# A transformer layer on eight cores: the load of the output-projection weights moved from the V-transpose stage to the attention block's start

## Chip, cores, metric
The kernel runs on all 8 cores of one Trainium2 chip. Each core runs the same program on its own 2048 tokens, with no exchange between cores. The metric is device time in microseconds of the slowest core.

## What is computed
One pre-norm transformer layer on x of shape (2, 8192, 2048): 16 heads of 128, rotary positions, attention within a window of 512, and an FFN of width 8192. The reference, cut:

```python
# attention on layernorm(x)
q, k, v = (einsum('bsi,oi->bso', xn, W) for W in (Wq, Wk, Wv))   # per head, 128 wide
q, k = _rope(q, cos, sin), _rope(k, cos, sin)
scores = einsum('bhnid,bhnjd->bhnij', qb, kw) * scale            # blocks of 512, keys of this and the previous block
base = (j > i) & (j <= i + WIN)
attn = softmax(where(mask, scores, -inf))
out = einsum('bhnij,bhnjd->bhnid', attn, vw)
x = x + einsum('bsi,oi->bso', out, Wo)
# FFN on layernorm(x)
D = gelu(X @ W0.T + bias0); x = x + (D @ W1.T + bias1)
```

## The kernel before
Each core works on 2048 own tokens plus 512 of context before them (CTX = 2560). The program is a row of blocks, each with code for the five engines, and each opened by `barrier`, which all five engines must reach. Within a block engines meet by counting semaphores. The blocks are:

- p0: layer norm of x and its transpose into `ln1T`.
- p1: projections Q, K and V (matmul at L370), spilled to HBM as `q_sp`, `k_sp` and `vT_sp`.
- p1t: the V-transpose stage (from L544). V was made transposed; here it is turned back. The 20 tiles of 128 tokens come in five groups (`sg4`) of four. GpSimd loads a group's 16 pieces of `vT_sp` into `vtl[sg4 % 2]` (L569); for groups 2 to 4 it first waits (`sTpV`) until TensorE is through with the group two before. TensorE waits for a group's 16 loads, then does 16 transposes per tile into `ptpv` (L606). ScalarE copies a tile to `vstage[st % 2]`, after the store of two tiles before has landed (`sSpVa`, `sSpVb`). SP stores the tile to `v_sp` (L586).
- p2: attention and output projection in four blocks (`qb`) of 512 tokens. Per block 64 steps of scores, exponential (ScalarE), scaling by the reciprocal and copy of the transposed result (VectorE), and product with V; then the projection with `wo_sb` (L799), the residual and the second layer norm. TensorE waits for `sRing` at the start of each block (10 DMAs: 4 for `kring`, 2 for `qring`, 4 for `vring`), and for `sWo2` (four wo loads) only after the attention of block 0.
- p3: the FFN in two stages (L1057, L1202), with weights streamed by GpSimd.

GpSimd issues its DMAs in program order on one queue; SP has another, and both run on the same 16 DMA engines. In p1t the function `wo_msk_load(g)` is called after group 1's vtl loads. It issues the mask load and four loads of `wo_t`, each 2 MB as written (bf16) and 4 MB as read (f32). `ring_kq(g, 0)` follows, then the vtl loads of groups 2 to 4, then `ring_v(g, 0)`. `wo_sb` and the rings have their own place in SBUF through p1t and p2. `DO_V` is true, so GpSimd in p2 issues only the ring loads of blocks 1 to 3, each after the attention of the block before (`sQbPE`).

Of the kernel before, what the change touches and what calls it, by code (L numbers as in the profile page):

```python
# [32 lines left out]
def build_nc():  # L33
# [3 lines left out]
    def dram_in(name, shape, dtype=F32):  # L37
        return nc.dram_tensor(name, shape, dtype, kind="ExternalInput").ap()
# [16 lines left out]
    msk_in = dram_in("msk", [128, 5 * 640], BF16)  # L55
# [24 lines left out]

    _wmap = {"q": wq_t, "ka": wk_t, "kb": wk_t, "va": wv_t, "vb": wv_t}
    WLOADS = [(_wmap[nm], oh) for nm, _, _, _ in SWEEPS for oh in range(2)]
    W1P = [0, 0]
    for li in range(len(WLOADS)):
# [4 lines left out]
    with ctx:  # L89
# [24 lines left out]
        sem = {n: e(nc.semaphore(n)) for n in semnames}  # L114
# [4 lines left out]
        def barrier(eng):  # L119
            eng.sem_inc(sem["sBar"], 1)  # L120
            eng.wait_ge(sem["sBar"], NENG * bar_n[0])
# [82 lines left out]
        with pA:  # L204
# [17 lines left out]
            with p0:  # L222
# [8 lines left out]
                with nc.Block() as blk:  # L231
                    @blk.sync
                    def _(s):
                        barrier(s)
                        s.dma_start(idm[:], idm_in).then_inc(sem["sMisc"], 16)
                        s.dma_start(ccs[:], cc_in).then_inc(sem["sMisc"], 16)
                        s.dma_start(sss[:], ss_in).then_inc(sem["sMisc"], 16)
                        for t in range(NT0):
                            if t >= 4:
                                s.wait_ge(sem["sLn1"], t - 3)  # L240
                            s.dma_start(xb[t % 4][:],
                                        x_ctx[t * 128:(t + 1) * 128, :]
                                        ).then_inc(sem[xsem[t % 4]], 16)
# [266 lines left out]
        msk = p2o.enter_context(nc.sbuf_tensor("msk_s", [128, 5 * 640], BF16))  # L510
# [5 lines left out]
        def ring_kq(g, qb):  # L516
            for o0 in range(0, 16, 4):
                g.dma_start(
                    kring[:, o0 * 1024:(o0 + 4) * 1024].rearrange(
                        "p (o c) -> p o c", c=1024),  # L520
                    k_spv[:, o0: o0 + 4, qb * 512: qb * 512 + 1024]
                ).then_inc(sem["sRing"], 16)
            for o0 in range(0, 16, 8):
                g.dma_start(
                    qring[:, o0 * 512:(o0 + 8) * 512].rearrange(
                        "p (o c) -> p o c", c=512),
                    q_spv[:, o0: o0 + 8, qb * 512:(qb + 1) * 512]
                ).then_inc(sem["sRing"], 16)

        def ring_v(g, qb):  # L530
            for j0 in range(0, 8, 2):
                g.dma_start(
                    vring[:, j0 * 2048:(j0 + 2) * 2048].rearrange(
                        "p (j f) -> p j f", f=2048),
                    v_spv[:, qb * 4 + j0: qb * 4 + j0 + 2, :]
                ).then_inc(sem["sRing"], 16)

        def wo_msk_load(g):
            g.dma_start(msk[:], msk_in).then_inc(sem["sMsk"], 16)
            for i0 in range(0, 16, 4):  # L540
                g.dma_start(
                    wo_sb[:, i0 * 2048:(i0 + 4) * 2048].rearrange(
                        "p (i f) -> p i f", f=2048),
                    wo_tv[:, i0: i0 + 4, :]  # L544
                ).then_inc(sem["sWo2"], 16)

        if DO_V:
            p1t = ExitStack()
            with p1t:
                vtl = [p1t.enter_context(  # L550
                    nc.sbuf_tensor(f"vtl{j}", [128, 16 * 512], BF16))
                    for j in range(2)]
                vstage = [p1t.enter_context(
                    nc.sbuf_tensor(f"vstage{j}", [128, 2048], BF16))
                    for j in range(2)]
                ptpv = [p1t.enter_context(
                    nc.psum_tensor(f"ptpv{j}", [128, 2048], BF16))
                    for j in range(2)]
                bar_n[0] += 1
                with nc.Block() as blk:  # L560
                    @blk.gpsimd
                    def _(g):
                        barrier(g)
                        for sg4 in range(5):
                            if sg4 >= 2:
                                g.wait_ge(sem["sTpV"], 4 * (sg4 - 1))
                            vs = sem["sVta" if sg4 % 2 == 0 else "sVtb"]
                            for o in range(16):
                                g.dma_start(  # L569
                                    vtl[sg4 % 2][:, o * 512:(o + 1) * 512],  # L570
                                    vT_sp[o * 128:(o + 1) * 128,
                                          sg4 * 512:(sg4 + 1) * 512]
                                ).then_inc(vs, 16)
                            if sg4 == 1:
                                wo_msk_load(g)
                                ring_kq(g, 0)
                        g.wait_ge(sem["sSpVa"], 16 * 4)
                        g.wait_ge(sem["sSpVb"], 16 * 4)
                        ring_v(g, 0)

                    @blk.sync
                    def _(s):
                        barrier(s)
                        for st in range(20):
                            s.wait_ge(sem["sEvV"], st + 1)
                            s.dma_start(  # L586
                                v_sp[st * 128:(st + 1) * 128, :],
                                vstage[st % 2][:]
                            ).then_inc(
                                sem["sSpVa" if st % 2 == 0 else "sSpVb"], 16)  # L590
                        s.wait_ge(sem["sSpVa"], 16 * 10)
                        s.wait_ge(sem["sSpVb"], 16 * 10)

                    @blk.tensor
                    def _(tn):
                        barrier(tn)
                        for sg4 in range(5):
                            tn.wait_ge(sem["sVta" if sg4 % 2 == 0 else "sVtb"],
                                       16 * 16 * (sg4 // 2 + 1))
                            for st4 in range(4):  # L600
                                st = sg4 * 4 + st4
                                if st >= 2:
                                    tn.wait_ge(sem["sEvV"], st - 1)
                                ins = None
                                for o in range(16):
                                    ins = tn.transpose(  # L606
                                        ptpv[st % 2][:, o * 128:(o + 1) * 128],
                                        vtl[sg4 % 2][:, o * 512 + st4 * 128:
                                                     o * 512 + (st4 + 1) * 128],
                                        idm[:])  # L610
                                ins.then_inc(sem["sTpV"], 1)

                    @blk.scalar
                    def _(scraw):
                        barrier(scraw)
                        sc = _AW(scraw)
                        for st in range(20):
                            sc.wait_ge(sem["sTpV"], st + 1)
                            if st >= 2:
                                sc.wait_ge(  # L620
                                    sem["sSpVa" if st % 2 == 0 else "sSpVb"],
                                    16 * (st // 2))
                            sc.copy(vstage[st % 2][:], ptpv[st % 2][:])
                            sc.sig(sem["sEvV"])

                    @blk.vector
                    def _(vraw):
                        barrier(vraw)
# [4 lines left out]
        with p2:  # L633
# [30 lines left out]
            with nc.Block() as blk:  # L664
# [34 lines left out]
                @blk.gpsimd  # L699
                def _(g):  # L700
                    barrier(g)
                    if not DO_V:
                        wo_msk_load(g)
                        ring_kq(g, 0)
                        ring_v(g, 0)
                    for qb in range(1, NQB):
                        g.wait_ge(sem["sQbPE"], qb)
                        ring_kq(g, qb)
                        ring_v(g, qb)
# [614 lines left out]
```

## Time and profile before

| what | us |
|---|---|
| runs of the kernel | 3915.23, 4255.12, 4403.44 (median 4255.12) |
| profiled execution | 3900.29 |
| its span, slowest core (3) | 3898.7 |
| spans of the eight cores | 3867.5 to 3898.7 |
| TensorE matmul busy | 3279.2 (84%) |
| VectorE, ScalarE busy | 786.2 each (20%) |
| GpSimd busy | 593.0 (15%) |

Read it so: one execution, core 3, times from the span's start. "PE" is TensorE's matmul, "PEld" its weight load. DMA share is the mean busy share of the core's 16 DMA engines; GB/s is what they wrote, so a load that turns f32 into bf16 counts with its bf16 bytes.

### The profile page before, as it was taken

Reading aid. Unit: us, or ns where it says so; the run is one execution under the profiler, and the core shown is the slowest. Engines: PE = TensorE matmul, PEld = TensorE weight load, DVE = VectorE, ACT = ScalarE, POOL = GpSimd, SP = SyncE. Lnnn points to the kernel's source line nnn. Section 1 sums busy time; section 2 is a strip of 40 time slices with the busy share of each in tenths; the row PEclk is TensorE's granted clock in tenths of the full one; section 3 lists DMA queues with packets and bytes.
Section 4 is the critical chain, followed back from the end, with each engine's and each line's share of the span. In section 5 each row is a group of like instructions: output and inputs, shape, how many; then the busy total and the mean of one; then the engine's idle time right before and its main releaser. Section 6 shows DMA issues by size and latency. Waiting matters only on the chain. (4 is left out here: it accounts for less than half of the span.)

```text
span 3898.7 us, 47168 instructions; the slowest of 8 cores (3867.5 to 3898.7 us)
## 1 busy us (share of the span) xinstructions
PE 3279.2 (84%) x17600; PEld 1633.4 (42%) x17600; DVE 786.2 (20%) x1618; ACT 786.2 (20%) x1285; POOL 593.0 (15%) x933
## 2 busy tenths in 40 slices
PE   1599999997157667676839999999997999999999
PEld 1344444443144353535424444444443444444444
DVE  5555554000024443434430000000000000000000
ACT  3355454111143241414201111111110000000000
POOL 1000101002110000000000000001203433343321
PEclk9999999998578888888859999999998999999999
DMA  9322555543931406050163333332807989889764
GB/s 234 102 62 62 101 103 106 99 86 95 232 130 55 163 1 216 1 189 28 60 167 76 81 81 81 81 78 62 152 39 178 223 200 223 211 218 225 189 198 126
DMA packets 191858, 488.96 MB, mean 125 GB/s; under 512 B 21776, under 2 KB 54544, under 8 KB 188816
## 3 DMA queue, kind: packets, MB, share of 16 engines
q0 software_dynamic: 132304, 304.97, 37.5%
q1 hardware_dynamic: 59328, 180.97, 14.0%
q8 instruction: 143, 2.34, 0.2%
q14 instruction: 83, 0.68, 0.1%
HBM read 487.96 MB, written 115.34 MB: 155 GB/s over the span
## 5 line engine op out<-in xcount | busy, mean ns | idle before, releaser
L1202 PE MATMUL pool<-w1q,gq 128*128 128x512 bf16 x4096 | 903.7, 382 | 42.0 <-DMA gq<-g_sp 38.5
L1057 PE MATMUL pool<-ln2T,w0b 128*128 128x512 bf16 x4096 | 886.2, 380 | 2.0 <-PEq L120 2.0
L370 PE MATMUL pool<-ln1T,wbuf 128*128 128x512 bf16 x3584 | 777.2, 380 | 6.6 <-PE pool L370 4.7
L1202 PEld LDWEIGHTS pool<-w1q,gq 128*128 128x128 bf16 x4096 | 397.6, 98 | 531.8 <-issue 68.7
L1057 PEld LDWEIGHTS pool<-ln2T,w0b 128*128 128x128 bf16 x4096 | 401.2, 98 | 486.9 <-issue 5.0
L370 PEld LDWEIGHTS pool<-ln1T,wbuf 128*128 128x128 bf16 x3584 | 350.5, 98 | 433.2 <-issue 13.8
L144 DVE TENSOR_TENSOR obuf<-pool,yh 128x512 f32<-128x512 f32 x64 | 44.3, 692 | 1806.1 <-PE pool L1206 1674.2
L1133 POOL DMA_DIRECT2D gq<-g_sp x256 | 225.4, 901 | 760.2 <-PE pool L1206 568.7
L170 ACT ACTIVATE gst<-pool,bias_s 128x2048 bf16<-128x2048 f32 x64 | 125.9, 1967 | 745.1 <-PE pool L1057 745.1
L799 PE MATMUL pool<-wo_sb,outT 128*128 128x512 bf16 x1024 | 238.8, 397 | 29.0 <-DVE ybuf L903 25.0
L828 ACT ACTIVATE expb<-pool 128x640 bf16<-128x640 f32 x256 | 180.2, 705 | 278.1 <-PE pool L742 275.2
L775 PE MATMUL ppv<-expT,vring 128*128 128x128 bf16 x1280 | 102.9, 248 | 117.2 <-DVE expT L870 117.2
L144 DVE RECIPROCAL rec<-sums 128x1 f32<-128x1 f32 x256 | 41.1, 160 | 699.6 <-ACT expb L828 697.1
L799 PEld LDWEIGHTS pool<-wo_sb,outT 128*128 128x128 bf16 x1024 | 102.6, 101 | 164.2 <-issue 55.9
L757 PE MATMUL ptp<-idm_s,expb 128*128 128x128 bf16 x1280 | 131.0, 241 | 44.6 <-DVE expT L870 40.4
L170 ACT COPY e2b<-pool 64x512 f32<-64x512 f32 x288 | 166.9, 580 | 6.9
L1028 POOL DMA_DIRECT2D w0b<-w_t x112 | 59.3, 605 | 676.6 <-PE pool L1057 614.7
L606 PE MATMUL ptpv<-idm_s,vtl 128*128 128x128 bf16 x320 | 33.9, 292 | 134.2 <-DMA vtl<-vT_sp 85.4
L144 DVE TENSOR_TENSOR tt<-e1b,ccs 128x512 bf16<-128x512 f32 x144 | 99.7, 692 | 219.2 <-ACTq L164 186.8
L775 PEld LDWEIGHTS ppv<-expT,vring 128*128 128x128 bf16 x1280 | 90.7, 112 | 126.7 <-issue 126.7
L314 PE MATMUL ptr<-idm_s,lnb 128*128 128x128 bf16 x320 | 37.3, 309 | 119.5 <-ACTq L164 119.5
L170 ACT COPY e1b<-pool 128x512 f32<-128x512 f32 x144 | 84.3, 585 | 231.3 <-PE pool L370 190.0
(59 smaller groups left out, 1969.3 us busy)
## 6 DMA issues: line engine op xcount, KB each, us to landing
gq<-g_sp POOLq DMA_DIRECT2D x256, 512.0 KB, 12.1
w0b<-w_t POOLq DMA_DIRECT2D x128, 256.0 KB, 16.4
g_sp<-gst SPq DMA_DIRECT2D x64, 512.0 KB, 2.6
w1q<-w_t POOLq DMA_DIRECT2D x256, 128.0 KB, 19.6
xb<-x_ctx SPq DMA_DIRECT2D x20, 1024.0 KB, 11.4
wbuf<-wk_t POOLq DMA_DIRECT2D x64, 256.0 KB, 17.5
wbuf<-wv_t POOLq DMA_DIRECT2D x64, 256.0 KB, 18.0
kring<-k_sp POOLq DMA_DIRECT2D x16, 1024.0 KB, 13.6
```

The costliest lines, as they stand in the source:

```text
L144: ins = fn(*a, **k)
L170: ins = fn(*a, **k)
L314: ins = tn.transpose(ptr[r][:, jj * 128:(jj + 1) * 128], lnb[t % 2][:, ic * 128:(ic + 1) * 128], idm[:])
L370: ins = tn.matmul(pool[:, slot * 2048 + k * 512: slot * 2048 + (k + 1) * 512], lhs, ln1T[:, roff: roff + 512], start=(i == 0), stop=(i == ...
L757: ins = tn.transpose(ptp[tp_slot][:, j * 128:(j + 1) * 128], expb[eb][:, j * 128:(j + 1) * 128], idm[:])
L775: ins = tn.matmul(pv[:, qx * 128:(qx + 1) * 128], vt, expT[hh % 2][:, col: col + 128], start=(jc == qx), stop=(jc == qx + 4))
L799: ins = tn.matmul(pool[:, hf * 1024 + col * 512: hf * 1024 + (col + 1) * 512], lhs, wo_sb[:, w0c: w0c + 512], start=(hx == 0), stop=(hx == ...
L828: scraw.activation(expb[eb][:], pool[:, ps_slot * 1024: ps_slot * 1024 + 640], AF.Exp, scale=SCALE, accum_out=sums[:, eb: eb + 1]).then_in ...
L1028: g.dma_start(w0b[ng % 2][:, i * 1024:(i + 1) * 1024], w0_t[i * 128:(i + 1) * 128, ng * 1024:(ng + 1) * 1024]).then_inc(ws, 16)
L1057: ins = tn.matmul(pool[:, slot * 2048 + scv * 512: slot * 2048 + (scv + 1) * 512], lhs, ln2T[:, i * TOWN + scv * 512: i * TOWN + (scv + 1) ...
L1133: g.dma_start(dstv[:, grp * 8:(grp + 1) * 8, :], gsrc).then_inc(gsem, 16)
L1202: tn.matmul(pp, lhs, w1q[hq4 % 2][:, n * 512: (n + 1) * 512], start=(n == 0), stop=False)
```

## The change
The mask load stays where it was. The four wo loads leave the V-transpose stage and become the first DMAs that GpSimd issues in the block p2, behind its barrier and ahead of the ring loads of block 1. `wo_msk_load` becomes `wo_load`, with the wo loop alone. No wait is added or removed, and nothing else changes.

```diff
-        def wo_msk_load(g):
-            g.dma_start(msk[:], msk_in).then_inc(sem["sMsk"], 16)
+        def wo_load(g):
             for i0 in range(0, 16, 4):
                 g.dma_start(
                     wo_sb[:, i0 * 2048:(i0 + 4) * 2048].rearrange(
@@ p1t, gpsimd
                             if sg4 == 1:
-                                wo_msk_load(g)
+                                g.dma_start(msk[:], msk_in).then_inc(
+                                    sem["sMsk"], 16)
                                 ring_kq(g, 0)
@@ p2, gpsimd
                     barrier(g)
                     if not DO_V:
-                        wo_msk_load(g)
+                        g.dma_start(msk[:], msk_in).then_inc(sem["sMsk"], 16)
                         ring_kq(g, 0)
                         ring_v(g, 0)
+                    wo_load(g)
                     for qb in range(1, NQB):
                         g.wait_ge(sem["sQbPE"], qb)
                         ring_kq(g, qb)
```

## Rows read from the trace of the kernel before

**Rows 1.** Medians of the two dies: span and mean granted TensorE clock.
```profile
die 0 (median of its cores): 3877.6 us, clock 0.935
die 1 (median of its cores): 3884.8 us, clock 0.932
```

**Rows 2.** The page's 40 slices of the span, in tenths.
```profile
PE   1599999997157667676839999999997999999999
...
DMA  9322555543931406050163333332807989889764
```

**Rows 3.** Timeline of TensorE, 925 to 1120: start, us, what [idle before <-releaser].
```profile
1063.05 3.57 PE L606 MATMUL ptpv<-idm_s,vtl 128*128 128x128 bf16 x32 [68.22 <-DMA vtl<-vT_sp]
...
1115.37 0.58 PE L727 MATMUL pool<-msk_s,idm_s 128*128 128x512 bf16 x1 [6.53 <-PEq L120]
```

**Rows 4.** Timeline of POOL (its DMA issues), 925 to 1120.
```profile
963.25 3.07 POOL L541 DMA_DIRECT2D wo_sb<-wo_t  x4
966.20 3.11 POOL L518 DMA_DIRECT2D kring<-k_sp  x4
...
970.94 8.67 POOL L569 DMA_DIRECT2D vtl<-vT_sp  x16
995.36 8.47 POOL L569 DMA_DIRECT2D vtl<-vT_sp  x16 [15.76 <-PE ptpv L606]
```

**Rows 5.** Issue and landing by line: msk, the last two wo, vtl group 2.
```profile
L539 POOL DMA_DIRECT2D msk_s<-msk x1: 607/607/607, 962.7 to 962.7; - x1
...
DMA to landing us min/median/max: 8.2/8.2/8.2
...
L541 POOL DMA_DIRECT2D wo_sb<-wo_t x2: 845/849/853, 964.7 to 965.5; - x2
...
DMA to landing us min/median/max: 57.4/63.8/70.3
...
L569 POOL DMA_DIRECT2D vtl<-vT_sp x16: 681/691/702, 970.9 to 978.9; - x16
...
DMA to landing us min/median/max: 82.7/83.3/83.9
```

**Rows 6.** Stretches: us, busy of PE, PEld, DVE, ACT, POOL, clock, DMA share, GB/s.
```profile
945.00:1063.00 118.00, 13.95 (x128) 12.38 (x128) 0.00 (x0) 16.20 (x9) 42.27 (x75) 0.51 0.98 227
...
1036.00:1063.00 27.00, 0.00 (x0) 0.00 (x0) 0.00 (x0) 0.00 (x0) 0.00 (x0) 0.50 1.00 315
```

**Rows 7.** Stores of vstage: 1002 to 1008, landings of all 20; ScalarE's copy after the hole.
```profile
L586 SPq DMA_DIRECT2D v_sp<-vstage x2: 319/319/319, 1002.3 to 1007.1; - x2
...
DMA to landing us min/median/max: 11.1/11.2/11.3
...
DMA to landing us min/median/max: 2.6/8.6/12.6
...
1065.06 1.86 ACT L170 COPY vstage<-ptpv 128x2048 bf16<-128x2048 bf16 x1 [58.14 <-PE ptpv L606]
```

**Rows 8.** SP's DMA queue, 960 to 1060: packets, MB, share of 16 engines.
```profile
q1 hardware_dynamic: 1152, 4.19, 11.1%
```

**Rows 9.** Timeline of TensorE, first output projection of block 0.
```profile
1247.90 4.29 PE L799 MATMUL pool<-wo_sb,outT 128*128 128x512 bf16 x10 [0.93 <-ACT outT L816]
```

**Rows 10.** Stretches after p1t; the instruction queues of 1120 to 1247, then of 3500 to 3600.
```profile
1120.00:1247.00 127.00, 87.66 (x947) 65.63 (x944) 58.48 (x189) 54.86 (x139) 0.00 (x0) 0.92 0.01 2
...
3500.00:3600.00 100.00, 100.00 (x459) 44.00 (x457) 4.84 (x7) 0.00 (x0) 42.30 (x64) 1.00 0.96 226
...
q8 instruction: 8, 0.13, 0.4%
q14 instruction: 6, 0.05, 0.1%
...
q8 instruction: 3, 0.05, 0.2%
```

**Rows 11.** VectorE's first operation in attention.
```profile
1118.94 0.16 DVE L144 RECIPROCAL rec<-sums 128x1 f32<-128x1 f32 x1 [450.68 <-ACT expb L828]
```

## Prediction
> **What bounds the kernel now.** I read the spans of the cores first, to see that no die is disturbed. The medians of the dies are 3877.6 and 3884.8 us at a clock of 0.935 and 0.932 [rows 1], so core 3, the slowest with 3898.7, can stand for all. Then the page's 40 slices: TensorE is busy to nine tenths nearly everywhere, and the deepest hole after the start is the eleventh slice (975 to 1072 us), where PE stands at 1 and the DMA row at 9 [rows 2]. The transpose stage of V (941 to 1115 us) lies around it, and the diff changes what is queued there.
>
> The timeline of TensorE in that stage shows the hole itself. The transposes of V get through groups 0 and 1 and then stand still for 68.22 us until 1063.05, released by a load of vtl. Attention starts at 1115.37 [rows 3]. Outside the hole the tiles go at the pace of the two-buffer rotation of the stores, whose landings take 2.6 to 12.6 us [rows 7].
>
> Next, what stands ahead of that vtl in the GpSimd queue. The timeline of POOL gives the order of issue: the four wo loads at 963.25, then kring (and, between, qring), and only then vtl of group 2 at 970.94 [rows 4]. The landings follow the same order. msk lands at 962.7 + 8.2 = 970.9 us; the last two wo loads at 964.7 + 57.4 = 1022.1 and 965.5 + 70.3 = 1035.8; vtl of group 2 last at 978.9 + 83.9 = 1062.8 [rows 5]. The DMA engines are busy all the time: share 0.98 from 945 to 1063 [rows 6]. They are what limits this stretch, and wo is in front.
>
> **What the change takes out of the stage.** Four DMAs (8.39 MB written as bf16, so 16.78 MB read as f32) leave the queue between msk and kring. I want the DMA time that is wo's own, without the stores that shared the engines meanwhile. The last store before the hole was issued at 1007.1 and landed about 11 us later [rows 7], so the last wo piece, from 1022.1 to 1035.8, ran alone: 13.7 us for 4.19 MB read. Four of them are 4 x 13.7 = 54.8 us. As a check from the other side: after wo, kring, qring and vtl of group 2 needed 1062.8 - 1035.8 = 27.0 us with no store beside them. In the changed order they start at 970.9 and share the engines with the stores. Eight stores moved 4.19 MB, and the stretch 960 to 1060 gives their queue 11.1% of 100 us [rows 8], so 11.1 us in all, some 2 of it before 970.9. That gives 970.9 + 27.0 + 9 = 1007 us for group 2, against 1063: 56 us. The two agree; I take 55.
>
> The Trainium skill would price wo otherwise: "HBM Reference", section "Specifications", gives a core about 358 GB/s when its neighbour streams too, which makes 16.78 MB an estimated 47 us and the kernel's time 3853 us. The alone piece ran at 4.19 MB / 13.7 us = 306 GB/s, so the trace has it slower than the page's share.
>
> **Bounds of that saving.** Above: wo held the queue from 970.9 to 1035.8, that is 64.9 us, if the stores in that time had cost nothing. Below: the next limit is the store rotation. Group 2's first copy needs the landing of the seventh store, issued at 1002.25 and landed near 1013.6 (11.3 us); its copy came at 1065.06 and took 1.86 [rows 7]. With stores no faster than beside wo, the gain is 1065.1 - 1013.6 = 51 us, and the second copy (1065.06 + 1.86 + 0.3 = 1067.2 against 1007.1 + 11.1 = 1018.2) makes it 49. The median over all 20 stores is 8.6 us, less than the 11 beside wo, so I keep 49 as the lower end only.
>
> **What stays in the stage.** msk, kring, qring and all of vtl keep their order. vtl of group 3 waits for the transposes of group 1, so it was issued at 995.36 [rows 4]; that is before 1007, so it still queues directly behind group 2. From group 2 on the traffic is the same as before, and I move the rest rigidly: attention starts at 1115.4 - 55 = 1060 us.
>
> **What the change adds.** The four wo loads are now the first thing POOL does in the attention block, at about 1060 us. Their issue takes 3.07 us [rows 4]. Only ring loads of block 1 are queued behind them, and those wait for the end of attention anyway. By their own rate they land at 1060 + 1 + 54.8 + a little for two xh loads of SP = about 1120 us. wo is first read at 1247.90 in the old time [rows 9], 1193 in the new. The cover is the attention of block 0, 132.5 us long, in which the DMA engines are at 0.01 of their time [rows 10]. The slack is some 70 us, so I cost the move at nothing. Without that cover it would cost its 55 us back.
>
> Does attention get slower with a stream of loads beside it? No row has attention and heavy loads together. The nearest row is the second FFN stage, where the DMA share is 0.96 and TensorE is busy for 100.0 of 100 us [rows 10]. So TensorE's work as such isn't slowed, which speaks for 0 as the lower bound; the upper one is 68 us, from the fetch rival below. I take 0, since the FFN row is the one with that traffic.
>
> **The sum.** The profiled execution: span 3898.7 us, 3900.3 with what lies around it. 3898.7 - 55 + 1.6 = 3845 us, which is 1.4% less. By the bounds 65 and 49 it is 3835 to 3851. The median of the three runs shown, 4255, is far above the profile and the lowest is 3915.2; I forecast for the profile's condition, so the low run would put the same saving at 3860.
>
> **Rivals.**
> Forecast, 0.80: 49 to 65 us are gained, 3835 to 3851.
> Part of the gain is lost, 0.09: the stage finds another limit before 1007 us is reached, or attention gives some of it back. For it speaks that the stores' rotation (49 us) is only a few us behind the loads (55 us). Against it speaks that all after group 2 is unchanged. Half lost is 3872.
> Nothing comes of it, 0.03: the loads of kring and vtl take up the time, as if all eight cores' reads were the limit. Then they would run slower than the 315 GB/s of 1036 to 1063 [rows 6]. 3900.
> Instruction fetches held up, 0.05, the case on the other side: in the 127 us of attention the instruction queues moved 14 packets [rows 10], about 6 in the 55 us of the load. A store that lands in 2.6 us at best needed 11 beside wo [rows 7], so a fetch could come 8.5 us later. 6 x 8.5 = 51 us would eat nearly the whole gain, and if 8 fetches are held it is 68, 13 us slower than before: 3913. It decides from 55 / 8.5 = 6.5 fetches. Against it: in the FFN stretch, 3 and more fetches at DMA share 0.96 cost PE nothing.
> wo comes late, 0.03: only if landing takes over 133 us from the start of attention, that is if the load runs at 40% of its rate; 3900 at 188 us. The Trainium skill names a cause ("SBUF — State Buffer", the "DVE blocks DMA" trap): VectorE in a two-port mode keeps GpSimd from writing descriptors, about 620 ns becoming 3100. By that factor the issue would be an estimated 15 us and the time unchanged at 3845 us. No row here has this overlap: VectorE's first operation comes 3.6 us after TensorE's first in attention [rows 11], when the issue is about over.
>
> **Range and chances.** The forecast's own range, 3835 to 3851, widened by the 15 us by which 3900.3 and 3915.2 differ, is 3820 to 3866. I reach to the half-lost case: 3822 to 3880, which leaves out about 0.15. A measurement of this kernel tells a difference of about 2%, 78 us, from none. Even the whole 68.2 us of the wait is less than that, so faster by over 2% is only left for the spread of executions: 0.06. Within 2%: 0.90. Slower by over 2% needs 133 us given back in attention: 0.04.
>
> **What would show it.** Right: POOL has no wo issue before the attention block; the wait for vtl of group 2 is 5 to 20 us, ended near 1007; attention starts near 1060 and its block 0 lasts 131 to 134 us; the wo loads land 55 to 62 us after their issue; everything later is earlier by the same 55. Wrong: TensorE idle with "issue" or its sequencer named in 1060 to 1120; a wait on wo before the first output projection; kring landing later than 22 us after msk; group 2's start released by ScalarE or the stores and not by vtl.

## The result and the profile after

The changed kernel takes 3856.85 us (median of 10 runs, lowest 3845.18) against 3918.63 us before (10 runs, lowest 3892.24). In some runs the cores of one die or of both (cores 0 to 3, 4 to 7) get a lower clock and take longer; the medians include four such runs of before and two of after, the ratios leave them out, and where a profile fell in such a run (e_six, e_double) I use the other die. The ratio is 0.9874, with a 95% interval of 0.9829 to 0.9918: 1.3% faster, between 0.8% and 1.7%. In us it is 49.3 (the means of the runs compared are 3908.0 and 3858.7). By the bound of 2% used in the prediction it counts as the same: the interval shows that there is a gain, and also that it is smaller than that bound. The profiled execution took 3855.9 us against 3900.3, 44 us less, with both dies alike:

```profile
die 0 (median of its cores): 3829.6 us, clock 0.940
die 1 (median of its cores): 3843.3 us, clock 0.937
```

Lines of the kernel after are those of core 3, the core of the rows of before, unless another core is named. First the timeline of TensorE in the V-transpose stage, which answers to [rows 3]:

```profile
956.60 3.57 PE L606 MATMUL ptpv<-idm_s,vtl 128*128 128x128 bf16 x32 [16.87 <-DMA vtl<-vT_sp]
...
1009.03 3.57 PE L606 MATMUL ptpv<-idm_s,vtl 128*128 128x128 bf16 x32 [20.45 <-DMA vtl<-vT_sp]
```

The wait for group 2 is down from 68.22 to 20.45 us, with the same releaser, and group 2 starts at 1009.03 in place of 1063.05. The timeline of POOL shows what was moved [rows 4]:

```profile
961.72 0.61 POOL L574 DMA_DIRECT2D msk_s<-msk  x1
962.24 3.07 POOL L518 DMA_DIRECT2D kring<-k_sp  x4
965.22 1.85 POOL L524 DMA_DIRECT2D qring<-q_sp  x2
966.97 8.63 POOL L568 DMA_DIRECT2D vtl<-vT_sp  x16
...
1064.76 2.98 POOL L540 DMA_DIRECT2D wo_sb<-wo_t  x4 [36.62 <-PEq L120]
```

The landings, by line (issue in us from the start, then min/median/max to landing) [rows 5]:

```profile
L574 POOL DMA_DIRECT2D msk_s<-msk x1: 607/607/607, 961.7 to 961.7; - x1
...
DMA to landing us min/median/max: 10.9/10.9/10.9
...
L568 POOL DMA_DIRECT2D vtl<-vT_sp x16: 637/652/664, 967.0 to 974.9; - x16
...
DMA to landing us min/median/max: 29.8/30.5/33.8
...
L540 POOL DMA_DIRECT2D wo_sb<-wo_t x4: 742/765/780, 1064.8 to 1067.0; - x4
...
DMA to landing us min/median/max: 20.5/38.0/55.1
```

vtl of group 2 lands at 974.9 + 33.8 = 1008.7, and wo at 1067.0 + 55.1 = 1122.1, some 76 us before TensorE first reads it at 1198.5. The stretches of the attention of block 0, with the wo loads beside it and without (us, busy of PE, PEld, DVE, ACT, POOL, clock, DMA share, GB/s) [rows 10]:

```profile
1065.00:1122.00 57.00, 41.62 (x403) 30.73 (x402) 24.83 (x81) 26.04 (x64) 2.74 (x4) 0.84 0.97 167
1122.00:1198.00 76.00, 51.06 (x560) 38.15 (x556) 34.63 (x112) 32.26 (x82) 0.00 (x0) 0.92 0.01 1
```

In the first stretch the DMA engines are full (0.97), and TensorE still does 403 matmuls in 57 us. On core 6 the granted clock of this stretch is 0.84 in both kernels. For the kernel before, the same stretch counted from the start of attention on core 6 (1119 to 1175, 56 us, DMA share 0.06) has 394 matmuls; the kernel after on core 6 (1059 to 1115, DMA share 0.97) has 395. On core 3 itself the kernel before had 411 matmuls in the like stretch (1116 to 1173), but at a granted clock of 0.92 against 0.84 after. These are the two lines of core 6, before and after:

```profile
1119.00:1175.00 56.00, 40.71 (x394) 29.92 (x395) 23.65 (x78) 25.11 (x61) 0.00 (x0) 0.84 0.06 20
```

```profile
1059.00:1115.00 56.00, 40.66 (x395) 29.95 (x393) 23.86 (x78) 25.38 (x63) 2.53 (x4) 0.84 0.97 170
```

To compare kernels below I use the medians over the eight cores of four marks, each the start of a first matmul, in us from the start of the span:

| kernel | group 2 | attention (first on kring) | first wo matmul | between the last two |
|---|---|---|---|---|
| before | 1062.2 | 1115.7 | 1249.2 | 133.1 |
| after | 1009.3 | 1064.4 | 1197.5 | 133.9 |
| difference | 52.9 | 51.3 | 51.7 | |

The start of the first FFN stage moves by 49.3 us (2046.5 to 1997.2), of the second by 51.7 us, and the median of the cores' last matmuls by 46.8 us. So most of the gain made in the V stage reaches the end, give or take a few us by which the later stages differ between executions.

What ends the stage, in both kernels, is the last store of V. On core 3 of the kernel after it is issued at 1060.9 and lands 2.9 us later, at 1063.8:

```profile
L586 SPq DMA_DIRECT2D v_sp<-vstage x1: 319/319/319, 1060.9 to 1060.9; - x1
...
DMA to landing us min/median/max: 2.9/2.9/2.9
```

The first matmul of the attention block (on the mask) starts at 1064.72. On the eight cores it comes 0.9 to 1.5 us after that landing, and vring has landed 10 us or more before. Before, on core 3, the last store landed at 1111.6 + 2.6 = 1114.2, and that matmul started at 1115.37.

### The profile page after: what moved, and what is told of

It is laid out like the page before. It is cut to its first block and busy times, and to the rows that moved or that the text cites. A ratio compares the mean times of both kernels' runs of the same rounds, so it can differ in the third digit from the quotient of the medians.

```text
span 3854.3 us, 47168 instructions; the slowest of 8 cores (3822.0 to 3854.3 us)
## 1 busy us (share of the span) xinstructions
PE 3279.7 (85%) x17600; PEld 1634.8 (42%) x17600; DVE 786.1 (20%) x1618; ACT 786.5 (20%) x1285; POOL 592.9 (15%) x933
## 5 line engine op out<-in xcount | busy, mean ns | idle before, releaser
L370 PEld LDWEIGHTS pool<-ln1T,wbuf 128*128 128x128 bf16 x3584 | 350.5, 98 | 433.1 <-issue 13.7
L728 PE MATMUL pool<-msk_s,idm_s 128*128 128x128 bf16 (+1 forms) x256 | 77.3, 302 | 60.1 <-DVE ybuf L904 29.2
```

The lines of the kernel that those rows point to most:

```text
L370: ins = tn.matmul(pool[:, slot * 2048 + k * 512: slot * 2048 + (k + 1) * 512], lhs, ln1T[:, roff: roff + 512], start=(i == 0), stop=(i == ...
L728: tn.matmul(pool[:, c0: c0 + mw], idm[:], mask_cols(qb, qc, 0), start=True, stop=False)
```

## Experiments

For e_six and e_double the cores of die 1 are used, against the same cores of before (group 2 at 1063.3, attention block 133.4 us) and after (attention block 133.8 us).

### e_half and e_six: what a wo load costs in the stage

Two of the four loads stay:

```diff
+                                wo_load(g, 0, 8)      # p1t, behind msk
-                    wo_load(g)
+                    wo_load(g, 8, 16)                 # p2
```

> Edit: two of the four wo loads stay in the V-transpose stage, two go to the attention block. Medians over the eight cores so far: start of the transposes of group 2 at 1062.2 us before, 1009.3 after; first attention step on kring 1115.5 and 1064.4. Theory A (the stage is limited by the DMA engines' work, and each piece costs its own share): group 2 at 1009.3 + 2 x 13.2 = 1036 us, attention at 1090. Theory B (the gain comes only when the queue ahead of group 2 is short enough, since the store rotation waits too): the first two pieces cost less than half, group 2 before 1028. Theory C (what counts is that nothing large stands in front, not how much): group 2 after 1045.

Group 2 starts at 1036.9 and attention at 1090.3; on core 2:

```profile
1035.65 3.21 PE L607 MATMUL ptpv<-idm_s,vtl 128*128 128x128 bf16 x32 [42.06 <-DMA vtl<-vT_sp]
```

From four to two pieces gains 25.3 us, from two to none 27.6. Theory A said 1036. No threshold shows: each piece costs about its own share. The run whose trace is read took 3883.9 us, between the two kernels.

The other way, two pieces more in the kernel before:

```diff
                                 wo_msk_load(g)
+                                for i0 in range(0, 8, 4):
+                                    g.dma_start(vring[...], wo_tv[:, i0: i0 + 4, :]
+                                    ).then_inc(sem["sDg"], 16)
                                 ring_kq(g, 0)
```

GpSimd waits for the two before it loads vring anew.

> Edit: the kernel before, with two more loads of the same kind (2 MB bf16 written, 4 MB f32 read each, into vring, which is loaded anew later) behind the four wo loads. No store shares the DMA engines by then, so this prices a piece alone. If a piece's own work is the 13.7 us that the prediction took from the last landing, group 2 starts at 1062.2 + 27.4 = 1089.6 us; if it is 12.7 us (a quarter of the 51 us that the queue's packets took in the kernel after), at 1087.6; if the stores' rotation were a limit beside it, less than 1085.

On core 5 the wait grows from 66.93 to 93.86 us:

```profile
1087.62 3.57 PE L614 MATMUL ptpv<-idm_s,vtl 128*128 128x128 bf16 x32 [93.86 <-DMA vtl<-vT_sp]
```

The median of die 1 goes from 1063.3 to 1086.8, 23.5 us for two pieces, or 11.8 each by the starts; by the waits of the four cores, which grow by 26.8, 26.9, 22.1 and 25.5 us, it is 11.1 to 13.5 each. The cores scatter by more than the two values that the expectation wanted to tell apart (12.7 and 13.7). The landings of the two added pieces settle it better. On core 5 the fourth wo load lands at 1034.8, and then:

```profile
L577 POOL DMA_DIRECT2D vring<-wo_t x2: 877/882/887, 965.0 to 965.8; - x2
...
DMA to landing us min/median/max: 82.8/88.9/94.9
```

That is 1047.8 and 1060.7, so 13.0 and 12.9 us for a piece with no store beside it. On the four cores of die 1 the two take 12.3 to 13.5 us each, 12.9 in the median. So the price goes on past four pieces, at 12.9 and not 13.7 a piece.

### e_double and e_mid: does the load cost anything beside attention

The four loads twice, one after the other, so that the stream lasts twice as long:

```diff
                     wo_load(g)
+                    g.wait_ge(sem["sWo2"], 4 * 16)
+                    wo_load(g)
@@ tensor, block 0
-                            tn.wait_ge(sem["sWo2"], 4 * 16)
+                            tn.wait_ge(sem["sWo2"], 8 * 16)
```

> Edit: the kernel after, with all four wo loads issued a second time in the attention block when the first four have landed, and the first output projection waiting for both. So some 105 of the 133 us of attention of block 0 have the DMA engines full. Theory A (attention takes nothing from the loads beside it): from the first kring matmul to the first wo matmul 132 to 135 us on the median core, as before (133.6) and after (133.3). Theory B (instruction fetches come late behind wo packets, 8.5 us each): the second 50 us hold up some 6 more, 20 to 50 us longer. Theory C (VectorE and ScalarE slowed a little by the stream): 2 to 5 us longer.

Attention to the first wo matmul takes 132.9 us on die 1 (133.8 with four loads, 133.4 with none), and 132.2 over all cores. The stretch on core 5, with the DMA engines full for 105 us:

```profile
1065.00:1170.00 105.00, 72.45 (x787) 53.63 (x786) 49.13 (x160) 48.65 (x121) 5.32 (x8) 0.92 0.98 163
```

The same 105 us of the kernel before on this core (1117 to 1222) had 761 matmuls at a DMA share of 0.04; the granted clock was 0.88 there and 0.92 here, so the two aren't quite like for like. On core 4 (1063 to 1168, and 1115 to 1220 before) it is 756 (clock 0.89) against 760 (0.92). So neither late instruction fetches nor a slower VectorE or ScalarE shows; theory A holds.

The loads in the middle of attention:

```diff
+                    g.wait_ge(sem["sExpN"], 12)
                     wo_load(g)
```

> Edit: the kernel after, with GpSimd waiting for the 12th scaled exponential before it issues the wo loads, so that VectorE is at work in its fast modes during the issue, and the loads come some 25 us later. Theory A (no lock worth the name): each issue takes 0.74 to 0.85 us, the loads last 50 to 53 us and are done some 50 us before the projection; attention 132 to 135 us. Theory B (VectorE keeps GpSimd from writing descriptors): issues of over 2 us each, first landing over 25 us after the issue; the end is still in time, so the kernel's time is the same.

On core 5 the issue starts at 1089.45, with VectorE at work:

```profile
L540 POOL DMA_DIRECT2D wo_sb<-wo_t x4: 740/756/770, 1089.5 to 1091.7; - x4
DMA to landing us min/median/max: 17.4/34.9/51.4
```

Each issue takes 0.74 to 0.77 us, as in the kernel after (0.742 to 0.780), and the last load lands 51.4 us after its issue. Attention to the first wo matmul takes 132.1 us, and the one run took 3846.0 us, within the runs of the kernel after. VectorE kept nobody waiting. The test is a mild one: in the 2.97 us of the four issues VectorE ran two scalings of 0.39 and 0.46 us, besides reciprocals and copies from PSUM, and the profile doesn't show its mode, so a hold-up as short as one such operation could pass unseen.

### e_nocover: the same loads with no work to hide them

```diff
-                    wo_load(g)
                     for qb in range(1, NQB):
                         g.wait_ge(sem["sQbPE"], qb)
+                        if qb == 1:
+                            wo_load(g)
```

> Edit: the kernel after, with the wo loads issued only when the attention of block 0 is through, ahead of the ring loads of block 1. Nothing covers them. Theory A (the move is free only for the cover, as the prediction says): group 2 at 1009 and attention at 1064 as in the kernel after, but TensorE waits some 52 us for wo, first wo matmul on the median core at 1197.6 + 50 = 1248 to 1252 us, and the kernel is back at the time of before, about 3905 us. Theory B (the gain was not the load's place but less crowding in the V stage): first wo matmul before 1230.

Group 2 and attention start as in the kernel after (1010.8 and 1064.2), the first wo matmul at 1250.5, and the one run took 3909.8 us. Core 3 waits:

```profile
PE pool L801 <- DMA wo_sb<-wo_t: 55.2, 1, 55.2
```

So the less crowded V stage alone is worth nothing at the end; the gain is the cover that attention gives. This agrees with the prediction's price for the case without it.

### e_tail and e_tail2: could the loads have stayed in the V stage, behind everything else

```diff
                         ring_v(g, 0)
+                        wo_load(g)          # p1t, last; e_tail2: two of the four
@@ p2
-                    wo_load(g)              # e_tail2: the other two
```

> Edit: the wo loads stay in the V-transpose stage, but as the last DMAs that GpSimd issues there, behind vring. Theory A (the later stores of V share the engines with wo, and land in some 11 us instead of 2.6 to 9.9): group 2 at 1009 as in the kernel after, attention 5 to 12 us later than its 1064.4. Theory B (the engines are idle enough by then, 0.85 busy): attention within 2 us of 1064.4, so that the place behind the barrier brings nothing of its own. wo lands near 1085 in both, long before the projection.

Neither theory was near for the start of attention. Group 2 starts at 1011.8, but attention at 1118.3, 54 us after the kernel after, and the one run took 3908.8 us. Core 3:

```profile
1117.42 0.59 PE L728 MATMUL pool<-msk_s,idm_s 128*128 128x512 bf16 x1 [60.64 <-PEq L120]
```

```profile
L540 POOL DMA_DIRECT2D wo_sb<-wo_t x4: 760/780/792, 1030.2 to 1032.4; - x4
DMA to landing us min/median/max: 41.4/63.3/81.5
```

```profile
L587 SPq DMA_DIRECT2D v_sp<-vstage x1: 320/320/320, 1070.6 to 1070.6; - x1
...
DMA to landing us min/median/max: 10.8/10.8/10.8
```

The last store landed at 1070.6 + 10.8 = 1081.4, and no instruction of the program waits for wo there. Yet TensorE sat 60.64 us, until 3.5 us after the last wo load had landed (1032.4 + 81.5 = 1113.9). On all eight cores the first kring matmul comes 3.9 to 4.2 us after that landing. So I formed another theory, that the end of a block waits for all that GpSimd's queue was given, and tried it with two loads there.

> Edit: two wo loads behind vring in the V-transpose stage, two at the start of the attention block. With all four behind vring, attention did not start until 3.9 to 4.2 us after the last wo load had landed, on each of the eight cores, though the last store had landed some 40 us before. Theory A (the end of a block waits until all that GpSimd's queue was given has landed): the second of the two loads lands near 1086 us, attention starts 4 us after it on every core, near 1090, as when the two stood ahead of kring (1090.3). Theory B (the stores of the last V tiles are what is late): attention follows the last store, near 1078 to 1082, before or without regard to the landing of wo.

```profile
L540 POOL DMA_DIRECT2D wo_sb<-wo_t x2: 760/768/775, 1030.6 to 1031.4; - x2
DMA to landing us min/median/max: 39.8/47.0/54.3
```

On core 3 the second load lands at 1031.4 + 54.3 = 1085.7 and attention starts at 1089.7. Per core, landing of the second load and first kring matmul:

| core | 0 | 1 | 2 | 3 | 4 | 5 | 6 | 7 |
|---|---|---|---|---|---|---|---|---|
| landing | 1086.2 | 1086.2 | 1086.4 | 1085.7 | 1083.5 | 1086.1 | 1086.1 | 1088.7 |
| attention | 1090.3 | 1090.1 | 1090.4 | 1089.7 | 1087.4 | 1090.1 | 1090.1 | 1092.6 |
| later by | 4.1 | 3.9 | 4.0 | 4.0 | 3.9 | 4.0 | 4.0 | 3.9 |

Theory A of e_tail2 holds, within 0.1 us of 4.0, over a spread of 5 us in the landings. The one run took 3879.4 us. That the loads had to go behind the block's barrier, and not only to the back of the queue, was not seen in the prediction. It is what makes this change worth something: with e_half's two pieces at the front and with e_tail2's at the back, attention starts at the same 1090.

### e_kqlate, e_kqsplit, e_three: what limits the rest of the stage

The 20.45 us wait that is left looks like the next gain. First, kring and qring moved behind all of vtl:

```diff
                             if sg4 == 1:
                                 g.dma_start(msk[:], msk_in)...
-                                ring_kq(g, 0)
+                        ring_kq(g, 0)       # after group 4's vtl, ahead of vring
```

> Edit: the kernel after, with the kring and qring loads of block 0 moved behind the vtl loads of group 4, ahead of vring. The wait of 17 to 23 us before group 2 should go. Theory A (the stage is limited by the DMA engines' total work, of which this removes nothing; they are busy 0.96 and 0.85 of the two halves of the stage): attention starts at most 5 to 8 us earlier than 1064.4, and the vring loads land later. Theory B (the wait itself is the cost): attention at 1045 to 1048, 17 us faster. Theory C: the rings land after the last store and attention waits for them, 0 to 10 us slower.

The long wait is gone (after the first wait, of some 17 us at 956, no core waits for vtl before 1002 us, and then for at most 4.67 us, on core 0), and attention starts at 1065.1: nothing gained (the time's ratio to before is 0.9843, 0.9788 to 0.9898, which can't be told from 0.9874). vring now lands late; on core 0:

```profile
L532 POOL DMA_DIRECT2D vring<-v_sp x4: 696/708/716, 1011.9 to 1014.0; - x4
DMA to landing us min/median/max: 34.3/41.1/46.2
```

It lands at 1060.2, and attention starts at 1064.0, 3.8 us later, by the rule found above; on the eight cores it is 3.8 to 4.0 us. The wait wandered from group 2 to the end of the stage. The bytes of the stage are the same, and though group 2 starts 22 us earlier (987.3), the last store lands only 3 us earlier on the median core (1059.9 against 1062.9).

Second, fewer bytes: the rings of heads 8 to 15 (3.1 MB) moved to the attention block.

```diff
-                                ring_kq(g, 0)
+                                ring_kq(g, 0, (0, 8))
@@ p2
+                    ring_kq(g, 0, (8, 16), "sRc")
                     wo_load(g)
@@ tensor
+                                if qb == 0 and step == 32:
+                                    tn.wait_ge(sem["sRc"], 16 * 3)
```

> Edit: the kernel after, with the loads of kring and qring for heads 8 to 15 of block 0 (3.1 MB) moved to the attention block, ahead of wo; TensorE waits for them at head 8. Theory A (DMA work in the stage is what counts): 3.1 MB at the 308 GB/s of kring, qring and vtl is 10 us less work; attention starts at 1054 to 1056, and the kernel is 8 to 10 us faster than after. Theory B (the store rotation is the next limit): 3 to 5 us. Heads 8 to 15 are not waited for: they land some 12 us after the start and are needed at 66 us.

Attention starts at 1055.2, 9.2 us earlier than after, as theory A has it. The time's ratio to before is 0.9834 (0.9778 to 0.9890), too wide to tell it from the kernel after by itself.

Third, `vstage` with three buffers in place of two.

> Edit: the kernel after with three vstage buffers in place of two. Theory A (DMA work limits the stage up to its last stores): group 2 starts within 2 us of 1009, attention 0 to 4 us earlier. Theory B (the rotation of the stores paces the tiles of groups 2 to 4): attention 8 us or more earlier.

Attention starts at 1059.5, 4.9 us earlier, with group 2 at 1009.5. That lies between the theories: the rotation costs a few us, and not the 8 of theory B. But here the limit has changed. The last store lands 6.1 us earlier than in the kernel after (1056.8 on the median core), and attention follows the landing of vring by 3.8 to 3.9 us on all eight cores. On core 3 vring lands at 1028.3 + 28.1 = 1056.4 and the first kring matmul comes at 1060.25:

```profile
L532 POOL DMA_DIRECT2D vring<-v_sp x4: 696/712/723, 1026.2 to 1028.3; - x4
...
DMA to landing us min/median/max: 14.6/21.4/28.1
```

So the end of the block took back about 1 us of what the third buffer gave.

### e_best: both together

```diff
+                                kr(g, 0, "sRing")     # kring heads 0 to 3
+                                qr(g, 0, "sRing")     # qring heads 0 to 7
@@ p2
+                    kr(g, 4, "sRc"); kr(g, 8, "sRc"); kr(g, 12, "sRc"); qr(g, 8, "sRc")
                     wo_load(g)
@@ tensor
+                                if qb == 0 and step == 16:
+                                    tn.wait_ge(sem["sRc"], 16 * 4)
@@ p1t: vstage[st % 3], one semaphore for each of the three
```

> Edit: the kernel after, and both things that gave something: only heads 0 to 3 of kring and 0 to 7 of qring are loaded in the V-transpose stage, the other 4.2 MB at the start of the attention block ahead of wo (TensorE waits for them at head 4), and vstage has three buffers. Theory A (DMA work and the store rotation add up as limits): 4.2 MB / 308 GB/s = 13.6 us less work, and the 5 us of the third buffer; attention starts on the median core at 1064.4 - 18 = 1046 us, against 1055.2 for the split alone and 1059.5 for the third buffer alone; the time is 3856.9 - 17 = 3840 us, 1.8 to 2% below before. Theory B (one of the two hides the other): attention at 1051 to 1055, 3847 us.

> The kernel after once more, on the same chip and beside the same runs of before as the version above. By its ten runs so far: 0.9874 of before, 1.0 to 1.7% faster; attention starts at 1064 on the median core.

e_best takes 3838.0 us, 0.9816 of before (0.9803 to 0.9830); the kernel after, beside the same runs of before, 3858.8 us, 0.9881 (0.9854 to 0.9909). The intervals don't meet: it is faster than both. Attention starts at 1046.4, 19.4 us before that run of the kernel after (1065.8), which is the difference of the times, 21 us, within 2 us. Theory A said 1046 and 3840. Core 3:

```profile
1046.26 0.59 PE L751 MATMUL pool<-msk_s,idm_s 128*128 128x512 bf16 x1 [13.98 <-PEq L120]
```

```profile
L546 POOL DMA_DIRECT2D vring<-v_sp x4: 696/712/723, 1012.0 to 1014.1; - x4
DMA to landing us min/median/max: 14.6/20.8/27.6
```

vring lands at 1014.1 + 27.6 = 1041.7, 4.6 us before the first matmul of attention and 5.0 before the first on kring. On the eight cores that last distance is 4.9 to 5.2 us, while the last store's varies more. So the landing of vring, with the end of the block behind it, is what comes next. Why it is 1 us longer here than in e_kqlate and e_three isn't known.

## Why the prediction was right

**What bounds the stage.** The wait of 68.22 us was indeed the queue ahead of vtl, and the DMA engines' work. e_half shows the price is paid piece by piece, and e_kqlate that moving the wait without moving bytes gains nothing: 3 us at the last store, which the end of the block then took back.

**The size.** I took 55 us and 51.3 came at the start of attention (52.9 at group 2); on core 3 alone, whose rows I used, it was 50.7 and 54.0. Two terms were a little off. The last piece of before, timed at 13.7 us between two landings, overstates a piece: e_six has 12.9, and four of those are 51.6 us in place of 54.8. In the kernel after, the queue with wo alone on it was busy for 80.8% of the 64 us from 1062 to 1126 on core 3, again 51.7 us or 12.9 a piece:

```profile
q0 software_dynamic: 2112, 8.39, 80.8%
```

(By its landings in attention, 1085.3 to 1122.1 on core 3, a piece took 12.3 us.) Why the fourth piece took 13.6 us or more on each of the eight cores of before is open. Being the last before kring isn't enough: the sixth piece of e_six has that place and took 12.3 to 12.9 us on die 1. The second way gave 1007 for group 2, and 1009.03 came. From msk's landing to that of vtl it is 1008.7 - 972.6 = 36.1 us, where I had 27.0 + 9 = 36.0. What was off is the starting point: msk landed 10.9 us after its issue and not 8.2. Why it is later with kring behind it in place of wo was not tried. That the two sums agreed within 1 us was in part luck, since one overstated a piece and the other took msk's landing too early. From group 2 to attention I moved everything rigidly. The marks of the table suggest a loss of 1.6 us there, but taken core by core the stage's rest lasts 54.0 us against 53.6 in the median, so nothing clear was lost; single cores differ by more (core 3: 55.7 against 52.3).

The Trainium skill ("HBM Reference", "Specifications") led to an estimated 47 us for wo; 16.78 MB in 51.7 us is 325 GB/s, between my 306 and its 358. A sum by that page would have been low by 4 us, mine was high by 4, both against the 51.3 at the start of attention.

**The bounds.** 49 to 65 us held for the start of attention (51.3), and barely for the times of the runs (49.3). They did not hold for the profiled executions, where 44 came. The lower end rested on stores as slow as beside wo; in the kernel after, TensorE's wait before group 2 is still released by vtl, as I had expected, and not by a store.

**The move costs nothing.** Right, and shown: the same matmul count beside a full DMA load, and 132 to 134 us of attention with none, with one load, with two in a row, and with the load in the middle. e_nocover shows the price without the cover: TensorE waits 52.3 to 56.5 us on the eight cores, and the time is 3909.8. What I had reasoned from the FFN rows, that heavy traffic doesn't hold TensorE, carries over to attention, where the chain of TensorE, ScalarE and VectorE is much tighter.

**The rivals.** Part of the gain lost: no. Nothing comes of it: no. Instruction fetches held: no; 105 us of full DMA engines left attention at 132.9 us. wo late: no; 76 us to spare, where I had some 70. The lock that the Trainium skill describes ("SBUF — State Buffer", the "DVE blocks DMA" trap) did not show with VectorE at work either: 0.740 to 0.770 us for an issue in e_mid. With the short operations there, this doesn't rule it out for other kernels.

**The signs.** POOL has no wo issue before attention, and TensorE waits for no wo load. The wait for vtl of group 2 was to be 5 to 20 us; on the eight cores it is 16.7 to 23.4. The last wo load landed 55.1 us after its issue, and kring 17.2 us after msk. One sign of being wrong came by its words: TensorE idle with its sequencer named in 1060 to 1120. It is the 8.81 us before attention's first matmul, at the barrier between the blocks; before the change the same wait was 6.53 us. It belongs to the end of the stage and should have been left out of the sign.

**The step that was missing.** I argued only for why the loads could go to the attention block, and held the place as one of several. e_tail shows that one block earlier there is none: what GpSimd has issued must land before the block ends. The forecast was safe from it, since vring had landed well before (at 1050.4 on core 3, 14 us before attention); the reasoning was incomplete, and that it did no harm here is luck.

**The time.** From a profiled execution of 3900.3 I forecast 3845, and the profiled execution of the kernel after took 3855.9: in the stated range of 3822 to 3880, but outside the forecast's own 3835 to 3851. Of the 11 us missing, 4 are missing at the start of attention. By the cores' last matmuls the gain is 46.8 us, so another 4 or 5 went after it, mostly in the second FFN stage: from its start to the last matmul it took 924.0 us on the medians, against 919.2 before. Its code is the same, and in the profiled executions of the other kernels it took 914 to 931 us (e_six and e_double left out), so I take this for scatter. The last 2 or 3 us are the difference between the slowest core and the median. The ratio, 0.9874 in place of the forecast 0.986, averages over more runs and gives 49.3 us.

## What to carry to other kernels

When a DMA queue is full and something waits on it, ask which of the bytes ahead are needed last, and count the bytes of the stage: reordering them moves the wait, taking them out of the stage shortens it by their own time. Put them where the DMA engines are idle and something long is computed without them, and check how long that cover is against the load. And look for the barrier between: a load that is to overlap the next block has to be issued in it.

## What the runs showed of the hardware and had not been expected

- The end of a block waits for the landing of all that GpSimd's queue holds. In e_tail and e_tail2, 16 cases in all, the next block's first kring matmul came 3.9 to 4.2 us after the last wo landing, with nothing in the program waiting for it; in e_kqlate and e_three 3.8 to 4.0 us after vring's, on all eight cores of each (there TensorE also waits for vring itself, but GpSimd's first issue in attention, which doesn't, came 3.3 to 3.5 us after the landing too). Where a store of SP landed last, as in the kernel after, it was only 0.9 to 1.5 us to the first matmul. That this is the queue's drain is an inference from these times; which instruction does it the profile doesn't show.
- A full DMA load costs a latency-bound chain of TensorE, ScalarE and VectorE nothing that can be seen: 394 and 395 matmuls in 56 us at DMA shares of 0.06 and 0.97.
- f32 loads that are turned into bf16 on the way went at 325 GB/s as read by the queue's busy time (51.7 us for 16.78 MB), or 341 by the 12.3 us between landings, with all eight cores loading.
